# The very last tile of a two-layer kernel made in two halves of 256 columns

## The reference

```python
def _rfs(xw, ab, AB, gs):
    dot_products = jnp.einsum('...d,rd->...r', xw, ab[:, None] * gs)
    correction = (0.5 * jnp.sum(xw * xw, axis=-1))[..., None] * (ab * ab)
    return 1.0 / math.sqrt(NUM_RFS) * AB * jnp.exp(dot_products - correction)

# layer 1: random features of x and of the weights, multiplied
attn = einsum('bsr,or->bso', _rfs(x, ...), _rfs(input_weights, ...))
x = _layernorm(x + attn)                       # called z in the kernel
# layer 2: two products, then the length of the pair
real = einsum('bti,io->bto', x, cos(theta + theta_noise))
imag = einsum('bti,io->bto', x, sin(phi + phi_noise))
x = _layernorm(x + sqrt(real * real + imag * imag))
```

## Time and profile before

| | us |
|---|---|
| median of 3 runs | 774.54 (774.42 to 775.04) |
| the profiled execution | 774.44 |
| its span, first to last instruction | 772.6 |
| PE busy in it | 750.4 (97%) |
| DVE busy | 496.8 (64%) |
| ACT busy | 373.2 (48%) |
| POOL busy | 179.0 (23%) |
| mean granted TensorE clock | 0.99 of full speed |

### The profile page before, as it was taken

The page is one execution under the profiler, slowest core; times in us unless marked ns, Lnnn a source line. Parts: engine busy times, 40 slices in busy tenths (PEclk is TensorE's granted clock), DMA queues, the critical chain, the costliest instruction groups (busy, mean ns, idle before and its releaser), DMA issues.

```text
span 772.6 us, 10427 instructions
## 1 busy us (share of the span) xinstructions
PE 750.4 (97%) x3396; PEld 617.8 (80%) x3396; DVE 496.8 (64%) x888; ACT 373.2 (48%) x643; POOL 179.0 (23%) x309
## 2 busy tenths in 40 slices
PE   9977989999999999999999999999999999999995
PEld 7855868888888888888888888888888888888884
DVE  4888684847648474674747567474755747576464
ACT  6824926263463616446362644527265462625322
POOL 4966030302112030211203012120201212030222
PEclk9998999999999999999999999999999999999998
DMA  8650050411404032140402214050231405010001
GB/s 277 213 178 0 1 177 1 118 59 46 131 27 149 0 99 78 41 136 21 155 0 79 97 41 136 10 166 1 73 104 41 136 0 162 15 62 6 28 28 54
DMA packets 32750, 60.75 MB, mean 79 GB/s; under 512 B 3168, under 2 KB 3168, under 8 KB 32736
## 3 DMA queue, kind: packets, MB, share of 16 engines
q1 hardware_dynamic: 32736, 60.60, 23.7%
HBM read 43.78 MB, written 16.81 MB: 78 GB/s over the span
## 4 chain that ended last, share of the span: by engine, by line
PE 86%; DVE 7%; ACT 3%; issue 2%; POOL 2%; POOLq 0%; DVEq 0%; ACTq 0%
PE token_ps L502 14%; PE token_ps L504 14%; PE token_ps L503 14%; PE project_ps L491 6%; PE project_ps L493 6%; PE project_ps L492 6%; PE token_ps L554 6%; PE token_ps L552 6%; PE token_ps L553 6%; PE turn_ps L560 3%; DVE stats L730 1%; DVE expo L653 1%; DVE trig L708 1%; DVE trig L712 1%; ACT F_raw L387 1%
## 5 line engine op out<-in xcount | busy, mean ns | idle before, releaser
L306 POOL TENSOR_TENSOR var_eps<-mv,eps 128x1 f32<-128x1 f32 x128 | 41.5, 324 | 568.1 <-DVE mv L734 568.0
L424 ACT ACTIVATE late<-token_ps 128x512 f32<-128x512 f32 x120 | 71.7, 598 | 131.5 <-PE token_ps L504 131.5
L416 ACT ACTIVATE zT_hi<-turn_ps 128x512 fp32r<-128x512 f32 x64 | 38.0, 598 | 182.2 <-PE turn_ps L560 182.2
L491 PE MATMUL project_ps<-xT_hi,gs_hi 128*128 128x512 f32 x248 | 102.1, 412 | 1.0 <-DVE xT_lo L648 0.7
L552 PE MATMUL token_ps<-W_hi,F_hi 128*128 128x512 f32 x256 | 99.7, 389 | 0.0
L554 PE MATMUL token_ps<-W_hi,F_lo 128*128 128x512 f32 x256 | 99.6, 389 | 0.0
L553 PE MATMUL token_ps<-W_lo,F_hi 128*128 128x512 f32 x256 | 99.6, 389 | 0.0
L648 DVE TENSOR_TENSOR xT_lo<-xT_raw,xT_hi 128x512 fp32r<-128x512 f32 x64 | 43.7, 690 | 85.9 <-ACT xT_hi L472 85.5
L493 PE MATMUL project_ps<-xT_hi,gs_lo 128*128 128x512 f32 x248 | 98.0, 395 | 0.0
L492 PE MATMUL project_ps<-xT_lo,gs_hi 128*128 128x512 f32 x248 | 97.4, 393 | 0.0
L745 DVE TENSOR_TENSOR late<-z,late 128x512 f32<-128x512 f32 x64 | 44.2, 691 | 81.9 <-ACT late L457 81.3
(11 more groups left out here) (126 smaller groups left out, 1333.2 us busy)
## 6 DMA issues: line engine op xcount, KB each, us to landing
xT_raw<-in_xT SPq DMA_DIRECT2D x16, 1024.0 KB, 5.9
x_tok<-in_x SPq DMA_DIRECT2D x16, 1024.0 KB, 7.0
out_tokens<-o_tile SPq DMA_DIRECT2D x64, 256.0 KB, 2.0
norm_bc<-token_norms SPq DMA_DIRECT2D x15, 256.0 KB, 3.6
trig<-in_gsT SPq DMA_DIRECT2D x4, 256.0 KB, 4.0
z<-in_wT SPq DMA_DIRECT2D x4, 256.0 KB, 4.7
trig<-in_theta_noise SPq DMA_DIRECT2D x4, 256.0 KB, 6.7
trig<-in_theta SPq DMA_DIRECT2D x4, 256.0 KB, 7.9
```

Of the source, the lines that this page charges most:

```text
L424: nc.scalar.activation(dst, bank[:, :], ACT.Square).then_inc(square_done, 1)
L491: nc.tensor.matmul(o, gs_hi[:, c, cols], rhs_hi[:, c, :], start=(c == 0), stop=False)
```

## The change

The sine products of the last tile of the last block, `phase(3, 1)`, become `last_phase`: 24 matmuls of 256 columns in place of 12 of 512. The 12 for the left 256 columns come first and go to the bank `project_ps0`, those for the right 256 columns go to `project_ps1`. Both banks are free by then, so PE waits for nothing there.

All that follows for this tile is made by half: the squares of the sine products, the sums of squares, the roots, the additions of z and the statistics. BN_AGGR then joins the two halves' statistics (`last_stats`). POOL's two instructions stay as they are. The normalisation and the store are in two halves too, and so there are two last stores of 128 KB in place of one of 256 KB. Nothing is changed in the 15 blocks before nor in the first three tiles of the last, but for one place in DVE's order, which is shown below.

```diff
+            step(NB - 2, 0, False)
+            for j in range(C - 1):
+                store_out(NB - 1, j)
+            for i, h in enumerate(HALVES):
+                sp.wait_ge(out_made, C * NB + i)
+                sp.dma_start(out_tiles[NB - 1][C - 1][:, h], o_tile[:, 1, h]).then_inc(out_stored[1], 16)
...
+                def last_tile_halves():                      # ACT
+                    for i, h in enumerate(HALVES):
+                        act.wait_ge(phase_done, 2 * C * NB + i)
+                        nc.scalar.activation(im2[:, 1, h], project_ps[i][:, h], ACT.Square).then_inc(square_done, 1)
+                    for i, h in enumerate(HALVES):
+                        act.wait_ge(sum_made, C * NB + i)
+                        nc.scalar.activation(mag[:, 1, h], re2[:, 1, h], ACT.Sqrt).then_inc(mag_made, 1)
...
+                def last_phase():                            # PE
+                    j = C - 1
+                    for bank, h in zip(project_ps, HALVES):
+                        o = bank[:, h]
+                        for c in range(C):
+                            s = slice(c * P, (c + 1) * P)
+                            nc.tensor.matmul(o, zT_hi[:, j, s], sin_hi[:, c, h], start=(c == 0), stop=False)
+                            nc.tensor.matmul(o, zT_hi[:, j, s], sin_lo[:, c, h], start=False, stop=False)
+                            last = nc.tensor.matmul(o, zT_lo[:, j, s], sin_hi[:, c, h], start=False, stop=(c == C - 1))
+                        last.then_inc(phase_done, 1)
...
+                    if not more and j == C - 1:              # DVE, in step
+                        moments(j - 1, stats2, mv2, mv2_made)
+                        norm2(b, j - 2)
+                        last_tile_halves()
+                        return
...
+            def last_tile_halves():                          # DVE
+                b, j, n = NB - 1, C - 1, C * NB
+                norm2(b, j - 1)
+                for i, h in enumerate(HALVES):
+                    dve.wait_ge(square_done, 2 * n + SQUARE_CREDIT + i)
+                    tt(re2[:, 1, h], re2[:, 1, h], im2[:, 1, h], ALU.add).then_inc(sum_made, 1)
+                for i, h in enumerate(HALVES):
+                    dve.wait_ge(mag_made, n + i)
+                    tt(y2[:, 1, h], z[:, j, h], mag[:, 1, h], ALU.add).then_inc(y2_made, 1)
+                    dve.wait_ge(y2_made, n + i)
+                    nc.vector.bn_stats(last_stats[:, i, :], y2[:, 1, h]).then_inc(stats2_made, 1)
+                dve.wait_ge(stats2_made, n + 1)
+                nc.vector.bn_aggr(mv2[:, j, :], last_stats[:, :, :]).then_inc(mv2_made, 1)
+                dve.wait_ge(out_stored[1], 32 * b + 16 + STORE_CREDIT)
+                dve.wait_ge(rstd2_made, n)
+                for h in HALVES:
+                    ts(o_tile[:, 1, h], y2[:, 1, h], mv2[:, j, 0:1], rstd2[:, j:j + 1],
+                       ALU.subtract, ALU.mult).then_inc(out_made, 1)
...
-            residual2(NB - 1, C - 1)
-            moments(C - 1, stats2, mv2, mv2_made)
-            norm2(NB - 1, C - 2)
-            norm2(NB - 1, C - 1)
```

More of the change, by code:

```diff
@@ L105, in build @@
         stats2 = sb("stats2", [P, C, 6])
+        HALVES = [slice(0, D // 2), slice(D // 2, D)]
+        last_stats = sb("last_stats", [P, 2, 6])
         mv2 = sb("mv2", [P, C, 2])
@@ L243, in _ @@
                     step(pair * 2 + slot, slot, True)
[L244 to L247, removed]
+            step(NB - 2, 0, False)
[4 more added lines that the diff above has]
+                sp.dma_start(out_tiles[NB - 1][C - 1][:, h], o_tile[:, 1, h]).then_inc(out_stored[1], 16)
+            sp.wait_ge(out_stored[0], STORE_CREDIT + 16 * NB * C // 2)
+            sp.wait_ge(out_stored[1], STORE_CREDIT + 16 * (NB * C // 2 + 1))
         @block.gpsimd
@@ L464, in step @@
                         act.wait_ge(mag_made, C * b + j - 1)
+                    if not more and j == C - 1:
+                        square(j, 0)
+                        magnitude(j - 1)
+                        last_tile_halves()
+                        return
                     for part in range(2):
@@ L633, in step @@
                     turn(3)
-                    for j, part in PHASE_ORDER[2:]:
+                    for j, part in PHASE_ORDER[2:-1]:
                         phase(j, part)
+                    last_phase()
             step(0, True, first=True)
```

## The result

| | before | after |
|---|---|---|
| median | 774.91 us (12 runs, 774.42 to 776.22) | 776.82 us (12 runs, 775.78 to 779.43) |
| profiled execution, its span | 774.44, 772.6 | 776.99, 774.9 |
| ratio to before | | 1.0023 (95% interval 1.0014 to 1.0031) |

The forecast was 775.3 with a range of 774.3 to 776.1 and "no change" as the likeliest. The measured time lies above the range, and the whole interval of the ratio lies above 1.

What follows compares the result with a forecast made beforehand. PE, busy 750.4 of 772.6 us, was taken to bound the kernel, so only the tail could move: +1.05 - 0.22 - 0.20 + 0.36 - 0.15 = +0.84 us, giving 775.3 us, range 774.3 to 776.1.

Steps and rivals of the forecast that it cites:

- the tail is a chain in which DVE has no slack at 765.3: After PE's last matmul, 8.0 us of span follow; DVE reaches tile 3 just when it is ready.
- a wait for POOL: On DVE, norm2 of tile 2 stands from 765.29 until POOL's root, done at 765.96, holding up tile 3's sums.
- a half instruction: In the tail, 256 columns cost 0.42 us on DVE and 0.41 for ACT's root, saving 0.2 to 0.27 each.
- PE's 24 narrow matmuls: Last sine product: 0.12 us apart, 2.88 against 2.72 us, hidden by DVE's wait up to a pitch of 0.191.
- The sum of the tail: All terms behind the last tile's first sine matmul together: +0.84 us.
- the start of BN_AGGR: Last tile on DVE: 769.24 in place of 768.19, +1.05 us from DVE's order and the doubled fixed parts.
- POOL gave back: POOL's instructions for tile 3: the first takes 0.19 us in place of 0.41, giving back 0.22.
- the normalisation of a half: Last tile: normalising 256 columns takes 0.35 us instead of 0.53 to 0.55 whole, saving 0.20.
- the end with its two stores: Last tile's stores on SP: second issue adds 0.36 us, smaller store lands 0.15 us sooner.
- Rival 1: Tail: halves overlap and DVE's order costs nothing; BN_AGGR at 767.30, 0.9 us earlier, total 773.3 us; chance 0.07.
- Rival 2: Last sine product: narrow matmuls 0.295 us apart pass their cover; PE ends 768.97, total 777.3 us; chance 0.08.
- everything before 761.73 us stays: All work ahead of the last tile's first sine matmul keeps its time, since PE's work there is unchanged.

Runs made afterwards that it cites:

- e3: The changed kernel with norm2 of tile 2 moved back behind BN_AGGR of the last tile, all halves kept; tail 10.60 us, ratio to before 1.0011.
- e4: The kernel before with only norm2 of tile 2 moved ahead of the last tile's sum of squares, nothing halved; tail 11.94 us, ratio 1.0022.
- e11: e2 with the last tile's sine product whole again, 12 matmuls of 512 columns, all behind it in halves; tail 11.73 us against 11.72.
- e1: The kernel before with only the unused buffer last_stats allocated where the change puts it; steady stretch 546.945 us, ratio to before 1.0012.
- e6: The changed kernel run again with nothing edited; steady stretch 546.945 us, tail 11.73 us, ratio to before 1.0027.
- e7: The kernel before with an unused buffer of 64 bytes per partition just ahead of ident; steady stretch 546.945 us, ratio to before 1.0010.
- e5: The kernel before run again with nothing edited, as a control; steady stretch 546.198 us, ratio to before 1.0003.
- e10: e2 unchanged, profiled a second time; steady stretch 546.198 us, tail 11.72 us.
- e12: e2 with one normalisation and one store of the last tile in place of two; tail 11.67 us.
- e2: The changed kernel with last_stats allocated behind all other buffers, so the others keep their old addresses; tail 11.72 us, ratio to before 1.0014.

## Why the prediction was wrong

**Right.** That the tail is a chain in which DVE has no slack at 765.3; that `norm2` of tile 2 ahead of the sums brings a wait for POOL (e3: 1.14 us less tail without it; e4: 1.01 more with it alone); that POOL's root shortens to 0.55 and its first instruction to 0.19, since nothing of DVE's runs beside them; that a half instruction costs about 0.42 (0.41 to 0.43 measured on DVE and for ACT's root); that PE's 24 narrow matmuls are covered (e11). The sum of the tail was +0.84; +0.82 was measured. That close a hit is partly luck: the start of BN_AGGR moved by +0.96 where +1.05 was forecast, POOL gave back 0.19 for 0.22, the normalisation of a half only 0.13 for 0.20 (it took 0.41, not 0.35), and the end with its two stores cost 0.18 for 0.21, so two misses of 0.09 and 0.07 cancel. Rival 1, that the order costs nothing, is what the halves would do without that wait: e3 shows that even then they gain 0.3, not the 1.1 that I gave it. There I had left out that POOL's contention comes back (0.2) and that the first sum cannot start before DVE is done with `norm2` of tile 1: in e3 it starts at 765.21 on the time axis of before, and BN_AGGR at 767.81 in place of rival 1's 767.30. Rival 2, the narrow matmuls passing their cover, did not happen: they start 0.120 apart, and the cover reached to 0.191.

**The step that failed** is the first: "The change leaves PE's work alone up to the sine products of the very last tile, so everything before 761.73 us stays." PE's instructions were the same, but one of their operands was not where it had been. The new buffer was allocated ahead of `ident` and moved it by 64 bytes, and the matmuls behind each turn became slower by 0.016 us per turn on average, 0.06 per block, 0.75 us in the steady stretch. e1, e3, e6 and e7 show it with four kernels, e4, e5, e10, e11 and e12 the other side. The description of the change has the same error: nothing is changed in the 15 blocks before as to instructions, but as to addresses it is. The term was in the change, in the line that allocates `last_stats`, which the diff printed above leaves out and e1 shows. I put it at nothing without a reason, and the trace of before alone holds no price for it.

**What the terms make.** 0.82 + 0.75 + 0.04 = 1.61 of the 1.91 us between the medians; the 0.04 is the stretch with the last six turns. The other 0.3 are within the interval (0.0009 of 775 us is 0.7). Nine turns stand ahead of the steady stretch, 0.14 us at 0.016 each by estimate, too little to be told from the scatter of the start; in the control e5 the kernel before stood at 1.0003 to itself.

Against the forecast, 775.28 with two digits, the 1.54 us are made of:

| | us |
|---|---|
| tail, less than forecast | -0.02 |
| slower matmuls ahead of the tail, missing in the forecast | +0.79 |
| base: the profiled execution of before lay below the later median of 774.91 | +0.47 |
| open | +0.3 |

The missing term is the largest. By itself it leads to 776.07, just inside the range; with the base or the open rest the time is outside. Without it, e2's ratio of 1.0014 is 776.0 us, inside as well. I had set the range by the terms of the tail alone and left no width for a change outside it.

## What to carry to other kernels

When an instruction is put ahead of others on an engine's queue, ask when its own inputs are ready, not only how long it takes: here a 0.5 us normalisation cost 1.0 to 1.1 us because its root was not there. A new buffer moves those behind it, and so can change stages whose code is untouched; allocate new ones last, so that nothing moves (which keeps the old time, not the best one: 128 bytes further was 0.17 us better here), and if time is lost where nothing was changed, compare a steady stretch of the busiest engine instruction by instruction. Halving a chain between engines saved only 0.3 us here, and one reason is that half an instruction cost 0.43 us where the whole one cost 0.69.

## What the runs showed of the hardware that was not expected

- Matmuls of 128x512 start 0.227 us apart in the steady stretch; behind the four 128x128 matmuls that turn a tile the first gap is 0.32 and the next ones are up to 0.236, for 5 to 10 matmuls. How much is lost there changes with the address of `ident`, which the turns read: 546.03 to 546.95 us for the same 2500 matmuls over seven placements. The reason is open.
- The same stretch repeats within 0.007 us between executions of one placement (eight of nine with `ident` unmoved or 256 bytes further, five of five with it 64 bytes further), while the start up to the 600th matmul varied from 153.9 to 155.9.
- Matmuls of 128x256, each with its own weights, start 0.120 apart, though a load of weights is recorded with 0.19: the recorded durations overlap.
